# A layer of windowed and full attention beside gated experts: masks laid by ScalarE, scores in alternating banks, one store of weights, query products among the global blocks

## The chip, the cores and the metric

One NeuronCore of a Trainium2 chip runs the whole layer. The metric is the device time of one execution in microseconds; lower is better. TensorE (PE in the profile; its weight loads are PEld), VectorE (DVE), ScalarE (ACT), GpSimd (POOL) and SyncE's DMA queue (SP) each run an instruction stream of their own in order, and meet at semaphores.

## What is computed

The input x is 8 sequences of 1024 tokens with 256 features. After a layer norm, two branches are added to it:

```python
qkv = x @ w_qkv + b_qkv                      # 16 heads of 16
scores = einsum('bhqd,bhkd->bhqk', q, k) * 16 ** -0.5
scores = where(mask, -inf, scores)           # 4 global heads: j > i; 12 local heads: j > i or i - j > 64
ctx = softmax(scores) @ v;  attn = ctx @ w_out + b_out
...
xV = einsum('btd,kdr->btkr', Q_side, V)      # 8 experts of rank 64
cum_yW = cumsum(einsum('btd,kdr->btkr', K_side, W), axis=1)
weights = softmax(gelu(Q_side @ router_w1.T + b1) @ router_w2.T + b2 + expert_bias)
out = einsum('btkr,kdr->btd', xV * cum_yW * weights[..., None], U) + weights @ b
out = out / n_valid                          # once "forward", once "inverse"
...
x = x + attn(xn) + (fwd + 0.5 * inv) @ W_O.T
```

## The kernel before

**Tiling.** Work goes by 16 chunks of 512 tokens, two a sequence; `c` is a chunk's half of its sequence, so even chunks have c = 0 and odd ones c = 1. A prologue folds the weight matrices. fp32 products are made of three fp32r matmuls of high and low parts (line 676), bf16 scores of three parts stacked in 96 or 99 rows.

**The order is written out by hand.** `Plan.add` appends stages to one list, and each engine's program walks that list and issues what belongs to it. So the order of `add` is the order of every engine's queue. `weave(main, side)` spreads the groups of `side` evenly between those of `main`. `uses=[...]` claims a PSUM bank or a buffer: the user of turn n waits (`take`, or a `seed`) until turn n - 1 has been read out, which `bank_read` counts.

**A chunk** has three stages on TensorE:

1. *Peaks and experts* (line 379 on). The largest score of each query is found first: `lpeak` (12 units, line 807) and `gpeak` (10 units in an even chunk, 26 in an odd one, line 821), each a bank of scores that VectorE reduces (lines 1222 and 1229, 0.62 us a piece). They rotate through banks 4 to 7. Local ones, and global ones on the diagonal, need a mask added. TensorE adds it by a matmul with the identity (line 801), or ScalarE copies it into the bank ahead of the scores (`seed`, line 1043), which then accumulate on it. Peaks are woven in blocks of four into the expert groups. Of these each j of 8 has: `x` (query product, bank 2, line 676), which ScalarE copies to `prod` (1027) and GpSimd multiplies by gate weights broadcast in `wide` (`weigh`, 1499); `c` (product over the running sum CH, bank 3), which VectorE multiplies in (`product`, 1305) and so frees bank 3 for the next `c`; ScalarE's rounded copy PH (1037), GpSimd's rest PL (1504); and `mix` (line 787) into the output banks 0 and 1. Query products 1 and 2 of the next chunk stand at the end of the global stage.
2. *Local blocks* (`local_groups`, line 235). Three groups of four heads, each in two halves: two `lscore` pairs (line 841) in banks 5 and 6, ScalarE's exponential (1055), GpSimd's masks on the first pair (1489, 1492); the second pair has a mask laid ahead by ScalarE (1048), but for the chunk's first, where TensorE does it (835). Then `lav` (line 866) sums into a context bank, group 1 and 3 in bank 7, group 2 in bank 4, and `ctx` on VectorE transposes it out (1321). Woven in: the next chunk's transposes, its key and query parts (ScalarE 986, VectorE 1193 to 1198), then its stacks are built by DMA (1587) and its four `hidden` products follow.
3. *Global blocks* (`global_groups`, 6 in an even chunk, 14 in an odd one): `gscore` (line 880) and `gav` (line 898) in bank 4, ScalarE's exponential (1063), GpSimd's mask on the diagonal (1482). Woven in: the next chunk's gates. VectorE turns them into weights, which SP stores by four 8 KB DMAs (1630) and reads back broadcast, two DMAs a `wide` buffer (1660). Also woven in: `values` in bank 2, and `finish` (909), the attention's output product for the chunk's first half of features. Behind the last block VectorE runs `ctx` (1321 to 1325), `cturn` (1333), ScalarE `chigh` (1069), VectorE `crest` (1338), and then product 0 of the next chunk.

## Time and profile before

| | us |
|---|---|
| device time, median of 3 runs | 1487.91 (1486.12 to 1490.52) |
| the profiled execution | 1491.34 |
| its span, first to last instruction | 1489.6 |
| TensorE busy in it | 1379.5 (93%) |
| VectorE, ScalarE, GpSimd busy | 989.5, 776.1, 586.5 |
| mean granted clock of TensorE | 0.989 |

A matmul's end is modelled and overlaps the next one's start, so the cost of work on TensorE is read from start to start. A row of the timeline has start, duration, engine, line, operation, tiles, shapes and count, and in brackets the idle time of the engine before it with what ended it.

### The profile page before, as it was taken

The page shows a single profiled execution, that of the slowest core. Times are in us where ns is not written, and L with a number is a line of the kernel's source. Part 1 is how long each engine was busy: PE and PEld are TensorE (multiplying, and loading weights), DVE is VectorE, ACT ScalarE, POOL GpSimd, SP SyncE. Part 2 cuts the span into 40 slices and gives each one's busy share as a digit, 9 for nine tenths or more (in the row PEclk, how much of TensorE's full clock was granted, in tenths as well). Part 3 has the DMA queues.
Part 4 walks back from the last instruction along what each step waited for, and adds up shares of the span by engine and source line. Part 5 has one row for each costly group of instructions (what it writes and reads, how often), then busy time and mean ns, then how long its engine had stood idle before and what let it go on. Part 6 is the DMA issues. An engine that isn't in the chain of part 4 may idle for free.

```text
span 1489.6 us, 35980 instructions
## 1 busy us (share of the span) xinstructions
PE 1379.5 (93%) x14481; PEld 1035.7 (70%) x14481; DVE 989.5 (66%) x2082; ACT 776.1 (52%) x1368; POOL 586.5 (39%) x663
## 2 busy tenths in 40 slices
PE   5978999999999999999999999999999999999996
PEld 4567685777758677586856778587775868667773
DVE  6667777567756777557875677566875578656661
ACT  2434537455464735645374554646356453755544
POOL 1025343453514444253433525144452534335341
PEclk9999999999999999999999999999999999999998
DMA  8430625326062541616353171624516153431610
GB/s 189 102 94 11 168 79 127 105 65 174 25 175 70 121 126 49 166 32 151 96 123 107 40 196 30 158 87 107 141 42 163 44 146 100 118 109 42 172 40 15
DMA packets 166614, 152.88 MB, mean 103 GB/s; under 512 B 37809, under 2 KB 149808, under 8 KB 166448
## 3 DMA queue, kind: packets, MB, share of 16 engines
q1 hardware_dynamic: 166448, 150.59, 38.8%
q8 instruction: 114, 1.87, 0.5%
q14 instruction: 52, 0.43, 0.1%
HBM read 108.57 MB, written 35.65 MB: 97 GB/s over the span
## 4 chain that ended last, share of the span: by engine, by line
PE 62%; DVE 15%; ACT 8%; issue 6%; DMA 4%; POOL 2%; SPq 1%; ACTq 0%; POOLq 0%; DVEq 0%
PE PS L676 30%; PE PS L787 11%; PE PS L821 4%; DVE rest L1193 3%; PE PS L880 3%; ACT HE L1063 3%; PE PS L807 3%; PE PS L909 3%; PE PS L898 2%; PE PS L963 2%; DMA weights_d<-weights_t 2%; DVE area L1198 2%; DVE area L1196 2%; ACT HE L1055 2%; ACT PS L1048 1%
## 5 line engine op out<-in xcount | busy, mean ns | idle before, releaser
L1504 POOL TENSOR_TENSOR PL<-prod,PH 128x512 fp32r<-128x512 f32 x128 | 164.7, 1287 | 201.3 <-ACT PH L1037 201.3
L676 PE MATMUL PS<-XH,WH 128*128 128x512 f32 x512 | 218.6, 427 | 21.7 <-ACT prod L1027 10.3
L1037 ACT ACTIVATE PH<-prod 128x512 fp32r<-128x512 f32 x128 | 80.8, 632 | 268.8 <-DVE prod L1305 252.8
L1499 POOL TENSOR_TENSOR prod<-prod,rest 128x512 f32<-128x512 f32 x96 | 124.8, 1303 | 242.9 <-DMA rest<-weights_d 166.6
L1229 DVE TENSOR_REDUCE block_peak<-PS 128x4 f32<-128x512 f32 x288 | 179.8, 685 | 48.0 <-PE PS L821 47.9
L676 PE MATMUL PS<-XH,WL 128*128 128x512 f32 x512 | 204.1, 399 | 0.0
L676 PE MATMUL PS<-XL,WH 128*128 128x512 f32 x512 | 203.6, 398 | 0.0
L1482 POOL TENSOR_SCALAR_AFFINE_SELECT HE<-HE 128x256 f32<-128x256 f32 x128 | 51.2, 406 | 364.2 <-ACT HE L1063 360.6
L1063 ACT ACTIVATE HE<-PS 128x512 f32<-128x512 f32 (+1 forms) x320 | 159.9, 553 | 33.5 <-PE PS L880 30.5
L1305 DVE TENSOR_TENSOR prod<-PS,prod 128x512 f32<-128x512 f32 x128 | 87.8, 686 | 97.3 <-PE PS L676 84.5
L676 PEld LDWEIGHTS PS<-XH,WH 128*128 128x128 f32 x512 | 97.1, 190 | 63.2 <-ACT prod L1027 16.8
L787 PE MATMUL PS<-UH,PH 128*128 128x256 f32 x512 | 133.8, 294 | 2.1 <-ACT PH L1037 2.1
L1027 ACT ACTIVATE prod<-PS 128x512 f32<-128x512 f32 x128 | 75.6, 590 | 113.2 <-PE PS L676 113.2
L1222 DVE TENSOR_REDUCE peak<-PS 128x4 f32<-128x512 f32 x192 | 119.9, 682 | 13.8 <-PE PS L807 13.8
L787 PE MATMUL PS<-UL,PH 128*128 128x256 f32 x512 | 128.3, 283 | 0.0
L676 PE MATMUL PS<-CH,WH 128*128 128x512 f32 x256 | 109.3, 427 | 12.4 <-DVE prod L1305 12.4
L1321 DVE STREAM_TRANSPOSE craw<-PS 128x512 f32<-128x512 f32 x64 | 45.4, 710 | 101.7 <-PE PS L898 95.5
L676 PEld LDWEIGHTS PS<-XH,WL 128*128 128x128 f32 x512 | 96.9, 189 | 22.5
L880 PE MATMUL PS<-area 99*128 99x256 bf16 (+1 forms) x640 | 101.1, 266 | 10.4 <-ACT HE L1063 7.3
L1055 ACT ACTIVATE HE<-PS 128x512 f32<-128x512 f32 x192 | 104.9, 593 | 6.9 <-PE PS L841 6.9
L676 PEld LDWEIGHTS PS<-XL,WH 128*128 128x128 f32 x512 | 98.0, 191 | 14.8
L787 PEld LDWEIGHTS PS<-UH,PH 128*128 128x128 f32 x512 | 97.7, 191 | 7.7 <-ACT PH L1037 3.8
(186 smaller groups left out, 3064.6 us busy)
## 6 DMA issues: line engine op xcount, KB each, us to landing
parts_d<-area SPq DMA_DIRECT2D x32, 768.0 KB, 5.0
area<-parts_d SPq DMA_DIRECT2D x128, 192.0 KB, 7.9
rest<-weights_d SPq DMA_DIRECT2D x192, 128.0 KB, 3.0
area<-parts_d SPq DMA_DIRECT2D x32, 576.0 KB, 7.8
tok<-in_L_attn_x_dram SPq DMA_DIRECT2D x16, 512.0 KB, 6.2
xt<-in_L_attn_x_dram SPq DMA_DIRECT2D x16, 512.0 KB, 4.1
wide<-weights_d SPq DMA_DIRECT2D x64, 128.0 KB, 3.0
out_dram<-xt SPq DMA_DIRECT2D x16, 512.0 KB, 3.8
```

What stands on the lines that cost most here:

```text
L676: ins = e.matmul(ps, a, b, start=first and k == 0, stop=last and k == n - 1, skip_group_check=True)
L787: ins = e.matmul(out_half(t), (PH, PL)[part][:, h, t * P:(t + 1) * P], u[:, j, :], start=False, stop=False, skip_group_check=True)
L880: ins = e.matmul(psum(i, lo=HALF * a + lo, hi=HALF * (a + 1)), KG[0:KSTK, g, j * P:(j + 1) * P], QS[0:KSTK, g, half * HALF + lo:(half + 1) ...
L1027: e.activation(prod[:, j % 3, :], psum(2), ACT.Copy).then_inc(bank_read[2])
L1037: e.activation(PH[:, h, :], prod[:, j % 3, :], ACT.Copy).then_inc(phi)
L1055: e.activation(HE[:, k, :], psum(i), ACT.Exp, scale=SCALE).then_inc(bank_read[i])
L1063: e.activation(two(HE[:, k, :], lo), two(psum(i), lo), ACT.Exp, scale=SCALE).then_inc(bank_read[i])
L1222: e.tensor_reduce(peak[:, t, 4 * grp:4 * (grp + 1)], psum(i).rearrange("p (a k) -> p a k", a=4), AX_X, ALU.max).then_inc(bank_read[i])
L1229: e.tensor_reduce(block_peak[ch % NC][:, t, :, j], psum(i).rearrange("p (a k) -> p a k", a=4), AX_X, ALU.max).then_inc(bank_read[i])
L1305: e.tensor_tensor(prod[:, r, :], psum(3), prod[:, r, :], ALU.mult).then_inc(bank_read[3])
L1499: e.tensor_tensor(prod[:, j % 3, :], prod[:, j % 3, :], wide[j % WIDE], ALU.mult).then_inc(weighed)
L1504: e.tensor_tensor(PL[:, j % 2, :], prod[:, j % 3, :], PH[:, j % 2, :].bitcast(F32), ALU.subtract).then_inc(plo)
```

## The change

- Peaks start their rotation of banks anew in each chunk. In every chunk but the first, three masks of the first four local peaks are laid by ScalarE, behind the previous chunk's last global scores; the fourth stays with TensorE.
- The first local mask is laid by ScalarE ahead of the chunk's last two expert groups, and each later one a step earlier. First pairs use bank 5, second pairs 6 and 4 in turn. All three local groups sum in bank 7. Peaks are woven into all expert groups but the last two (17 instead of 19 groups behind the first, in a middle chunk).
- Query products 1 and 2 of the next chunk, and `finish` of the first half, stand among the global blocks; the first `values` stands before the last AV block in bank 7, the second behind it. The three `weigh` follow one another on GpSimd at the end.
- The gates' weights go out in one DMA of all 128 partitions (128 KB), and `wide` reads each row as two halves.
- The last global scores of a chunk, and the values, write their whole bank as TensorE sees it (scores are 256 wide instead of 128), since masks laid by ScalarE are accumulated on.
- In the first chunk, the next chunk's norm comes in one piece behind the first two peak blocks.

```diff
--- before.py
+++ after.py
@@ -112,7 +112,7 @@
     def ctx_bank(grp):
-        return 7 if grp % 2 else 4
+        return 7 if grp else 4
@@ -180,7 +180,7 @@
     def add_values(ch, u):
-        add_on("values", ch, u, uses=["bank2" if ch else f"bank{2 + u}"])
+        add_on("values", ch, u, uses=[("bank7", "bank2")[u] if ch else f"bank{2 + u}"])
         if u == T // 2 - 1:
@@ -235,15 +235,15 @@
         units = [(grp, half) for grp in range(1, 1 + NL // 4) for half in range(2)]
-        scores = [(ch, grp, half, pair, score_use()) for grp, half in units for pair in range(2)]
+        scores = [(ch, grp, half, pair, f"bank{6 - 2 * (n % 2) if pair else 5}") for n, (grp, half) in enumerate(units) for pair in range(2)]
+        masks = [[(add_seed, bank, "lscore", *key)] for *key, bank in scores[1::2]]
         order = []
         for n, (grp, half) in enumerate(units):
-            order.append([(add_lscore, *scores[2 * n]), (add_lscore, *scores[2 * n + 1])])
-            if n + 1 < len(units):
-                order[-1].append((add_seed, scores[2 * n + 3][4], "lscore", *scores[2 * n + 3][:4]))
+            order.append(masks[n + 1] if n + 1 < len(units) else [])
+            order[-1] = order[-1] + [(add_lscore, *scores[2 * n]), (add_lscore, *scores[2 * n + 1])]
             if n:
                 order[-1].append((add_lav, ch, *units[n - 1]))
-        return order
+        return order, masks[0]
@@ -258,7 +258,7 @@
         for j in range(2 * KB):
-            if j < 2 * KB - 1 and (j > 1 or not ch):
+            if 1 < j < 2 * KB - 1:
                 order.append([(add_x, ch, j + 1, part) for part in range(2)] + [(add_weigh, ch, j + 1)])
@@ -308,11 +308,12 @@
         c = ch % NC
+        turns["peak"] = 0
         order = [[(add_lpeak, ch, t, grp, peak_use())] for t in range(T) for grp in range(NL // 4)]
...
         for n, ((stage, *key),) in enumerate(order + gpeaks):
-            if stage is add_lpeak and n >= PEAKS:
+            if stage is add_lpeak and (n >= PEAKS or ch and n < PEAKS - 1):
                 masks[n].append((add_seed, key[-1], "lpeak", *key[:-1]))
@@ -320,11 +321,9 @@
         order += gpeaks
-        if ch == 0:
-            add_norm(1, order)
         blocks = range(0, len(order), PEAKS)
         joined = lambda groups, n: [stage for group in groups[n:n + PEAKS] for stage in group]
-        return [joined(order, n) + joined(masks, n + PEAKS) for n in blocks]
+        return [joined(order, n) + joined(masks, n + PEAKS) for n in blocks], joined(masks, 0)
@@ -379,17 +378,30 @@
         add_c(0, 0, part)
+    for part in range(2):
+        add_x(0, 1, part)
+    add_weigh(0, 1)
...
-        experts, peaks = expert_groups(ch), peak_groups(ch)
+        experts = expert_groups(ch)
+        peaks = next_peaks if ch else peak_groups(ch)[0]
         split = len(experts) - (0 if nxt else 4)
...
             experts[1].append((add_finish, ch - 1, 1))
-            experts[2], experts[3] = experts[3], experts[2]
-        run(experts[0] + peaks[0])
-        weave(experts[1:split], peaks[1:])
+        experts[2], experts[3] = experts[3], experts[2]
+        if ch:
+            run(experts[0] + peaks[0])
+        else:
+            run(peaks[0] + [(add_x, 0, 2, part) for part in range(2)] + [(add_weigh, 0, 2)] + peaks.pop(1))
+            for n in range(len(NORM)):
+                add("norm", 1, n)
+            run(experts[0])
+        weave(experts[1:split - 2], peaks[1:])
+        locals_, first_mask = local_groups(ch)
+        for group in [first_mask] + experts[split - 2:split]:
+            run(group)
         if ch:
@@ -402,7 +414,7 @@
             side = [[(add_rows, ch, 1)]] + experts[split:] + [last_mix]
-        weave(local_groups(ch), side)
+        weave(locals_, side)
         add_lav(ch, NL // 4, 1)
@@ -414,33 +426,36 @@
         order = global_groups(ch)
-        side = []
         if nxt:
-            first_x, first_c = ([(add, ch + 1, 0, part) for part in range(2)] for add in (add_x, add_c))
-            run(first_x + order[0] + first_c)
+            x0, x1, x2 = ([(add_x, ch + 1, j, part) for part in range(2)] for j in range(3))
+            run(x0 + order[0] + [(add_c, ch + 1, 0, part) for part in range(2)])
             add("logits", ch + 1, uses=["bank7"])
             add("chigh", ch, 0)
+            if ch + 2 < CHUNKS:
+                add_norm(ch + 2, order[1:-2])
+            steps = 2 + 3 * (ch % NC)
+            last = len(order) // 2 - 1
+            order[1] += [(add_gates, ch + 1), (add, "crest", ch, 0)]
+            for n, other in ((0, [(add_gate_parts, ch + 1)]), (steps // 2, x1), (steps, x2), (steps + steps // 2, [(add_finish, ch, 0)]),
+                             (last - 1, [(add_values, ch + 1, 0)])):
+                order[2 * n + 2] += other
+            next_peaks, first_masks = peak_groups(ch + 1)
+            order[2 * last] += first_masks
             order = order[1:]
-            if ch + 2 < CHUNKS:
-                add_norm(ch + 2, order)
-            side = [[(add_gates, ch + 1)], [(add_gate_parts, ch + 1)]] + [[]] * (2 * (ch % NC))
-            side += [[(add_values, ch + 1, 0)], [(add_values, ch + 1, 1)]]
-            side[0].append((add, "crest", ch, 0))
         else:
             add("crest", ch, 0)
-        side.append([(add_finish, ch, 0)])
-        weave(order, side)
+            order[len(order) // 2].append((add_finish, ch, 0))
+        for group in order:
+            run(group)
         if nxt:
+            add_values(ch + 1, 1)
             add("stacks", ch + 1, "global")
-        if nxt:
-            add_weigh(ch + 1, 0)
-            run([(add_x, ch + 1, 1, part) for part in range(2)])
-            add_weigh(ch + 1, 1)
         add("cturn", ch, 1)
...
         if nxt:
-            run([(add_x, ch + 1, 2, part) for part in range(2)])
-            add_weigh(ch + 1, 2)
+            for j in range(WIDE):
+                add_weigh(ch + 1, j)
         add("crest", ch, 1)
@@ -529,7 +544,7 @@
         peak_d = [nc.dram_tensor(f"peak_d_{n}", (3 * k, C), BF16, kind="Internal").ap() for n, k in (("local", NL), ("global", NG))]
-        weights_d = nc.dram_tensor("weights_d", (2 * KE, C), F32, kind="Internal").ap()
+        weights_d = nc.dram_tensor("weights_d", (P, HALF), F32, kind="Internal").ap()
         rows_d = nc.dram_tensor("rows_d", (3, 2 * KE, C), BF16, kind="Internal").ap()
@@ -717,7 +732,7 @@
                             pairs += [(xh, wh), (xh, wl), (xl, wh)]
-                        ins = mms(psum(i, lo=a * D, hi=(a + 1) * D), pairs)
+                        ins = mms(psum(i, lo=a * D, hi=(a + 1) * D), pairs, first=a == 0)
                     ins.then_inc(values_ps)
@@ -872,7 +887,7 @@
                     i, _ = where[stage]
-                    lo = max(0, (j - c * T) * P - half * HALF)
+                    lo = max(0, (j - c * T) * P - half * HALF) if (j, half) != tiles(c)[-1] else 0
                     q.wait_ge(peak_in[1], 16 * (ch + 1))
@@ -1288,7 +1303,7 @@
                     q.wait_step()
-                    q.wait_ge(weights_out, 16 * 4 * ch)
+                    q.wait_ge(weights_out, 16 * ch)
                     q.wait_ge(rows_cast, ch)
@@ -1624,10 +1639,7 @@
                         q.wait_ge(wide_in[i], 16 * 2 * (use(f"wide{i}", "wide", ch, i) - 1))
-                    for w in range(2):
-                        for h in range(2):
-                            row = 32 * (2 * w + h)
-                            e.dma_start(weights_d[KE * w:KE * (w + 1), h * HALF:(h + 1) * HALF], weights_t[row:row + KE, :]).then_inc(weights_out, 16)
+                    e.dma_start(weights_d, weights_t[:, :]).then_inc(weights_out, 16)
                     q.wait_ge(rows_cast, ch + 1)
@@ -1646,7 +1658,7 @@
                     ch, j = key
-                    q.wait_ge(weights_out, 16 * 4 * (ch + 1))
+                    q.wait_ge(weights_out, 16 * (ch + 1))
                     if j >= WIDE:
@@ -1656,8 +1668,11 @@
                             q.wait_ge(bias_in, 16 * 15)
+                    by_half = weights_d[2 * 32 * (j // KB):2 * 32 * (j // KB + 1), :].rearrange("(h e) t -> e h t", h=2)
                     for k in range(2):
-                        e.dma_start(wide[j % WIDE][R * k:R * (k + 1), :], weights_d[2 * j + k:2 * j + k + 1, :].to_broadcast([R, C])).then_inc(wide_in[j % WIDE], 16)
+                        n = 2 * (j % KB) + k
+                        e.dma_start(wide[j % WIDE][R * k:R * (k + 1), :].rearrange("p (h t) -> p h t", h=2), by_half[n:n + 1].to_broadcast([R, 2, HALF])).then_inc(wide_in[j % WIDE], 16)
```

## Rows read from the trace of the kernel before

**Rows 1.** Busy time of each engine, share of the span, instructions (the page).

```profile
PE 1379.5 (93%) x14481; PEld 1035.7 (70%) x14481; DVE 989.5 (66%) x2082; ACT 776.1 (52%) x1368; POOL 586.5 (39%) x663
```

**Rows 2.** Windows of chunks 6 and 7: stretch and length, busy us, clock, DMA.

```profile
624.01:702.35 78.34, 75.53 (x819) 59.38 (x818) 53.47 (x117) 42.66 (x74) 33.78 (x38) 1.00 0.38 96
702.35:798.21 95.86, 90.20 (x979) 65.84 (x978) 65.08 (x137) 52.09 (x92) 39.27 (x43) 1.00 0.42 114
```

**Rows 3.** TensorE's waits by releaser: us in total, times, longest.

```profile
PE PS L676 <- DVE prod L1305: 12.4, 10, 3.1
PE PS L841 <- ACT PS L1048: 11.8, 18, 0.7
...
PE PS L676 <- ACT prod L1027: 10.3, 15, 0.7
```

**Rows 4.** Timeline of TensorE, handover from chunk 7 to 8.

```profile
782.30 0.39 PE L676 MATMUL PS<-WH,XH 128*128 128x256 f32 x1
...
783.85 0.61 PE L880 MATMUL PS<-area 99*128 99x256 bf16 x4
...
790.77 0.39 PE L909 MATMUL PS<-OH,PH 128*128 128x256 f32 x1
...
792.31 0.40 PE L880 MATMUL PS<-area 99*128 99x128 bf16 x4
...
793.99 0.41 PE L898 MATMUL PS<-HE,Va 128*17 128x128 f32 x8 [0.73 <-POOL HE L1482]
...
796.69 0.50 PE L676 MATMUL PS<-XH,WH 128*128 128x512 f32 x1 [0.69 <-ACT prod L1027]
...
798.20 0.39 PE L801 MATMUL PS<-peak_mask_l,ident_b 128*128 128x512 bf16 x1
...
800.86 0.50 PE L676 MATMUL PS<-CH,WH 128*128 128x512 f32 x1
```

**Rows 5.** The same, four peak blocks without a mask of TensorE's, chunk 7.

```profile
708.78 1.08 PE L807 MATMUL PS<-area 96*64 96x128 bf16 x32
709.80 0.50 PE L676 MATMUL PS<-XH,WH 128*128 128x512 f32 x1
```

**Rows 6.** The same, the mask of the first local scores, chunk 7.

```profile
743.54 0.38 PE L835 MATMUL PS<-mask_l,ident_b 128*128 128x512 bf16 x1
743.77 0.40 PE L841 MATMUL PS<-area 99*128 99x64 bf16 x8
```

**Rows 7.** Timeline of VectorE, handover from chunk 7 to 8.

```profile
794.49 0.72 DVE L1321 STREAM_TRANSPOSE craw<-PS 128x512 f32<-128x512 f32 x1 [10.11 <-PE PS L898]
...
797.40 1.16 DVE L1338 TENSOR_TENSOR PL<-craw,PH 128x512 fp32r<-128x512 f32 x1 [0.70 <-ACT PH L1069]
798.48 0.68 DVE L1305 TENSOR_TENSOR prod<-PS,prod 128x512 f32<-128x512 f32 x1
```

**Rows 8.** Timeline of ScalarE, masks of the third block of peaks, chunk 7.

```profile
710.51 2.40 ACT L1043 ACTIVATE PS<-peak_mask_l 128x512 f32<-128x512 bf16 x4 [0.93 <-DVE peak L1222]
```

**Rows 9.** Timelines of TensorE and GpSimd, handover from chunk 6 to 7.

```profile
695.88 0.40 PE L880 MATMUL PS<-area 99*128 99x128 bf16 x4
...
705.75 0.50 PE L676 MATMUL PS<-CH,WH 128*128 128x512 f32 x1 [0.69 <-DVE prod L1305]
...
703.36 2.84 POOL L1499 TENSOR_TENSOR prod<-prod,rest 128x512 f32<-128x512 f32 x2 [5.94 <-DMA rest<-weights_d]
```

**Rows 10.** The chain that ended last, at that handover: start, us, what.

```profile
694.43 5.04 DMA weights_d<-weights_t
```

**Rows 11.** Window over the stacks' transfers: as rows 2; last are DMA share, GB/s.

```profile
684.00:697.00 13.00, 12.82 (x117) 8.63 (x116) 7.11 (x30) 10.08 (x20) 2.78 (x7) 1.00 1.10 235
```

**Rows 12.** Timelines of VectorE and TensorE, local blocks of chunk 7.

```profile
759.70 0.71 DVE L1321 STREAM_TRANSPOSE craw<-PS 128x512 f32<-128x512 f32 x1
...
758.83 0.31 PE L866 MATMUL PS<-HE,Vs 128*17 128x64 f32 x8 [0.48 <-POOL HE L1492]
...
763.86 0.50 PE L676 MATMUL PS<-XH,WH 128*128 128x512 f32 x1 [0.18 <-DVE rest L1193]
```

## The prediction, made before the changed kernel ran

> **What bounds the kernel now.** I read the page's busy times first: TensorE is busy for 93% of the span, every other engine far less [rows 1]. The windows by chunk come next: they show that an even chunk (first half of a sequence, few global blocks) takes 78.3 us and an odd one 95.9, with the granted clock at full, and that TensorE is busy for 75.5 and 90.2 of them [rows 2]. So TensorE's order of work is the time, and only three things can move it: work taken from it, waits taken from it, and waits given to it. Its waits by releaser are short and regular [rows 3]: ten for VectorE's product (12.4), fifteen, one a handover, for ScalarE's copy of a query product (10.3), eighteen for a mask laid by ScalarE (11.8). Then I read the three places that the change touches, row by row: the handover from the global blocks to the next chunk, the local blocks, and the first peaks.
>
> **Masks.** A block of four peak units with TensorE's own masks takes 800.86 - 798.20 = 2.66 us [rows 4], one without 1.02 [rows 5]: 0.41 a mask. 45 of them go (three in each chunk but the first), 18.5 us. A local mask takes the 0.23 us between its start and that of what follows [rows 6]; 16 go, 3.7 us. The last global scores grow from 0.40 to 0.61 [rows 4], 16 x 0.21 = 3.4 us more. If TensorE were never late for anything else, that alone would be 19 us. But each handover's masks lie just before the first product over CH, which waits for bank 3, and that for VectorE's product 0. So I follow who is ready when.
>
> **Handover odd to even** (7 of them). Count from the start of the last global scores. Before: 800.86 - 792.31 = 8.55 us to the first CH product [rows 4]. In it are 0.73 for GpSimd's mask, 0.69 for ScalarE's copy, two query products, the peak block with four masks. After: the wider scores and one AV block (about 1.1), the first half of the values (783.85 - 782.30 = 1.55 [rows 4]), which covers the 0.73, and the last AV block (0.35, the gap from its start to the query product's, bounded by the row's 0.41), done at about 3.1. TensorE then has the other values (1.5) and the first peak block with one mask (1.02 + 0.41): it is through at about 6.0. VectorE however still has its whole chain behind the last AV block: from the context's transpose (794.49) to the end of product 0 (798.48 + 0.68) are 4.67 us [rows 7], and the three masks (0.60 each [rows 8]) and a values copy stand before ScalarE's link of that chain, some 0.3 more. So bank 3 is free at about 8.1: **the masks, the POOL wait and the copy's wait go, and about 2 us of waiting for product 0 come.** Gain 0.45. Ahead of it two query products of 1.51 (798.20 - 796.69 [rows 4]) come in and two values go out: even. Net -0.5; bounds: -1.7 if ScalarE's queue costs nothing and the products fill waits among the global blocks, +0.4 if GpSimd's three multiplications in a row stretch VectorE's links (a subtraction beside one took 1.16, the equally wide next operation 0.68 [rows 7]). Times 7: -3.5 us.
>
> **Handover even to odd** (8). Before 705.75 - 695.88 = 9.87 us, the finish product (1.54, from 790.77 to 792.31 [rows 4]) in it [rows 9]. VectorE's chain would now end after 8.1 to 8.7 here too, but the stretch before it has finish and the two query products in and values out: +1.5. That is 0.2 or so gained or lost. The second condition is the weights: product 0 started when GpSimd's multiplication released it, and that when the broadcast rows landed [rows 9]. The last 8 KB store took 5.04 us to land [rows 10]: the DMA engines are at 1.10 of their time from 684 to 697 [rows 11], with the stacks issued before it. One store instead of four saves a microsecond of issue, into a queue that is full anyway; it carries 128 KB instead of 32, at 235 KB/us [rows 11] 0.4 us more. I take +0.15 beyond what the local stage adds, between -1.6 and +1.0; times 8: +1.2.
>
> The Trainium skill, "DMA: Bandwidth & Descriptors", section "Rules for kernel authors", says to coalesce small transfers into one, because below 64 KB mostly overhead is paid; the 5.04 us of a store of 8 KB agree that size is not what it pays for. Its section "Anatomy of one DMA" puts a DMA at about 2.0 us and its bytes at 436 GB/s: by that the single store would take an estimated 2.3 us.
>
> **Local blocks.** All three groups now gather in bank 7, where the second used bank 4. The first AV block of group 3 must wait until VectorE has transposed group 2 out of it. Before, that transpose ran from 759.70 to 760.41, behind the key parts in VectorE's queue, while that AV block started at 758.83 [rows 12]. So it starts 1.6 us later; behind it in TensorE's queue stand query parts, the last AV block and the hidden products. Those waited for VectorE themselves: the second hidden product started at 763.86 as released by VectorE [rows 12], and without that wait 0.8 us of the 1.6 remain. The alternating bank 4 takes away the 0.7 us waits for a mask (11.8 [rows 3]); but ScalarE runs the same exponentials, masks and copies there and is full, so what is late next is ScalarE itself, and AV blocks start as before. Even: +0.85. In odd chunks the last product of the experts was held up behind peaks on VectorE; with the peaks laid a group earlier about 0.5 is won: +0.3. Bounds 0 and +1.2. 8 x 0.85 + 7 x 0.3 = +8.9. In the last chunk VectorE's queue is empty there: 0.
>
> **First peaks of odd chunks.** Peaks are woven into fewer expert groups: 9 blocks into 17 where there were 19. The third block then comes right after one query product, at about 711.3 (709.80 [rows 5] + 1.51), not after the mix. Its four masks were laid from 710.51 to 712.91 [rows 8]; its fourth unit can't start before 712.9, where it would have at 712.1. 0.9 us each with its tail, 7 chunks: +6.3; bounds 0 and +1.2. The last chunk has that order already; its peaks get denser still: +1.
>
> **First chunk.** Some 6.9 of the 12.4 us of waits for products are there (the eight handovers to odd chunks have about 0.69 each [rows 9]). The new order puts chunk 1's whole norm ahead of product 0 on VectorE, and takes it out from between later products: -1.5, bounds -5 and +3.
>
> **Sum.** -3.5 + 1.2 + 8.9 + 6.3 + 1 - 1.5 = +12.4 us on the profiled execution (1491.34, span 1489.6), which is 3.4 us over the median; on the median 1487.91 that is 1500.
>
> **Rivals.** (a) **The gains land**: VectorE and ScalarE are early enough after all and TensorE's ledger is the time: masks -22.2, copy waits -10.3, POOL waits 7 x 0.73, scores +3.4, that is -34; with half of it lost to the chain, 1471. For it speaks 93% busy; against it the 4.67 us chain, which I find no way around. 0.18. (b) **The bank wait is absorbed**: the transposes come earlier in VectorE's queue, or later waits swallow it. Then the local stage is at -0.5 in odd chunks and 0 in even ones: 12.4 - 8.9 - 3.5 = 0, 1488. 0.14. (c) **One store lands early**, by the rule above, as a mechanism here: weights at hand some 2.5 us sooner, and VectorE's chain alone decides in the 8 even handovers; it is worth 0.4 each: 1497. Against it stands the full queue [rows 11]. 0.08. (d) **GpSimd's row of multiplications**: from the point where the first starts before the context's normalisation ends, that operation and the following ones take up to 0.5 to 0.7 longer at 15 handovers: 1500 + 10 = 1510, slower. The 1.16 speaks for it [rows 7], that ScalarE holds the chain meanwhile against. 0.10. The forecast itself has 0.50.
>
> The Trainium skill, "SBUF — State Buffer", section "SBUF: two separate sides", calls the port pair that VectorE and GpSimd share an exclusive lock held for a whole instruction; by that rule (d) would happen wherever a VectorE operation with two SBUF inputs meets a multiplication, and the 1.16 agrees.
>
> **How the numbers follow.** About 0.3% (4.5 us) is what a measurement of this kernel can tell from no change. Slower: forecast 0.50 less 0.04 for its lower end, (c) 0.08 less 0.02, (d) 0.10: 0.62. Same: (b) 0.14 and 0.02 from the edges: 0.16. Faster: (a) 0.18 and 0.04 of the low ends: 0.22. The terms' bounds taken half together give 1488 to 1509; the range goes to 1480, into (a), and to 1511 for (d).
>
> **What would show it.** Right: TensorE waits of about 2 us for VectorE's product 0 at every handover; AV blocks of the third local group waiting for VectorE's transpose; a wait for ScalarE's masks of 0.3 to 0.9 in the third peak block of odd chunks; the ACT copy waits gone; the store landing no sooner than the stacks. Wrong: even chunks under 78 us and odd ones under 95.5, which would mean that VectorE's chain starts or runs earlier than its row says.

## The result, and the profile after

The changed kernel takes 1539.12 us (median of 4 runs, 1537.46 to 1542.07) against 1487.01 of the kernel before beside it: ratio 1.0352, 95% interval 1.0322 to 1.0381. It is slower, as forecast, but by 52 us and not by 12, and outside the range. The profiled execution took 1540.33, span 1538.6. Lines of the code after are 15 higher than before from the matrix helper on (L676 is now L691).

Busy times and TensorE's waits (releaser, us in total, times, longest), where [rows 1] and [rows 3] stood:

```profile
PE 1385.8 (90%) x14420; PEld 1054.1 (69%) x14420; DVE 980.0 (64%) x2082; ACT 797.6 (52%) x1429; POOL 580.4 (38%) x663
```

```profile
PE PS L691 <- DVE prod L1320: 47.3, 23, 9.3
PE PS L881 <- DVE craw L1336: 44.7, 30, 2.3
...
PE PS L856 <- ACT HE L1070: 8.7, 16, 1.1
...
PE PS L822 <- ACT PS L1058: 1.8, 10, 0.2
```

The fifteen waits for ScalarE's product copy and the eighteen for its masks at the local scores are gone, but for one of 0.3 us, as the change meant. In their place stand 47.3 us for VectorE's products and 44.7 for its context transposes. But TensorE also has 61 instructions fewer and is busy for 6 us longer. The windows by chunk (columns as in [rows 2]) show why: the granted clock, 1.00 in both before, is 0.98 and 0.97.

```profile
638.61:721.23 82.62, 75.98 (x816) 60.45 (x815) 55.50 (x118) 44.47 (x80) 33.52 (x38) 0.98 0.41 103
721.23:819.32 98.09, 91.38 (x976) 67.81 (x975) 63.95 (x136) 53.12 (x96) 38.49 (x44) 0.97 0.40 103
```

TensorE at the handover from chunk 7 to 8, as in [rows 4], the same product behind chunk 8, and the window just behind the first of them:

```profile
814.70 0.61 PE L895 MATMUL PS<-area 99*128 99x256 bf16 x4
...
818.00 0.38 PE L691 MATMUL PS<-WH,XH 128*128 128x256 f32 x1
...
820.74 0.41 PE L822 MATMUL PS<-area 96*64 96x128 bf16 x8
823.38 0.50 PE L691 MATMUL PS<-CH,WH 128*128 128x512 f32 x1 [2.23 <-DVE prod L1320]
...
824.23 0.63 PE L691 MATMUL PS<-CH,WH 128*128 128x512 f32 x1
...
906.38 0.80 PE L691 MATMUL PS<-CH,WH 128*128 128x512 f32 x1 [2.51 <-DVE prod L1320]
```

```profile
824.11:827.52 3.41, 3.41 (x15) 3.02 (x14) 2.72 (x5) 2.24 (x4) 1.24 (x1) 0.50 0.50 154
```

From the last scores to the first product over CH (tokens) are 8.68 us (8.55 before), 2.23 of them a wait. Then the same matmul takes 0.63 us instead of 0.40: the granted clock has dropped to its lower level, 1.2 GHz, and stays there for 3.41 us. The trace has 7 such stretches before, one of them between chunk 0 and the last chunk, and 26 after. In the middle chunks each stands in or just behind a wait: the one above, at 12 of the 15 handovers, or one of those in the local blocks, where TensorE waits for VectorE to transpose contexts out of their bank (`craw`):

```profile
953.86 0.42 PE L881 MATMUL PS<-HE,Vs 128*17 128x64 f32 x8 [1.13 <-DVE craw L1336]
...
963.55 0.31 PE L881 MATMUL PS<-HE,Vs 128*17 128x64 f32 x8 [1.42 <-DVE craw L1336]
```

The wait alone does not settle it. At the handover to chunk 14 it is 2.23 us too, and the clock behind it stays at 1.00:

```profile
1367.70 0.50 PE L691 MATMUL PS<-CH,WH 128*128 128x512 f32 x1 [2.23 <-DVE prod L1320]
```

```profile
1367.70:1371.11 3.41, 3.41 (x32) 3.01 (x34) 3.41 (x6) 3.20 (x6) 1.30 (x1) 1.00 0.69 180
```

By phases of the trace, as a mean of a chunk (seven even, seven odd; "head" is from the first peak scores, without a mask ahead of them, to the first local scores or their mask, and has the end of the handover in it):

| us | head even, odd | local even, odd | global even, odd | chunk 0 | last chunk |
|---|---|---|---|---|---|
| before | 36.01, 41.07 | 25.33, 26.28 | 17.00, 28.94 | 89.89 | 86.00 |
| after | 39.30, 43.37 | 26.78, 27.55 | 16.51, 27.27 | 92.67 | 89.45 |

### The profile page after: what moved, and what is told of

Its sections match the earlier page's. It is cut to its first block, busy times and chain, and to the rows that moved or that the text cites. A ratio compares the mean times of both kernels' runs of the same rounds, so it can differ in the third digit from the quotient of the medians.

```text
span 1538.6 us, 35861 instructions
## 1 busy us (share of the span) xinstructions
PE 1385.8 (90%) x14420; PEld 1054.1 (69%) x14420; DVE 980.0 (64%) x2082; ACT 797.6 (52%) x1429; POOL 580.4 (38%) x663
## 4 chain that ended last, share of the span: by engine, by line
PE 66%; DVE 17%; ACT 6%; issue 5%; DMA 4%; POOL 2%; SPq 0%; ACTq 0%; DVEq 0%; POOLq 0%
PE PS L691 32%; PE PS L802 11%; PE PS L836 4%; PE PS L881 3%; PE PS L895 3%; PE PS L913 3%; PE PS L924 3%; DMA weights_d<-weights_t 2%; ACT HE L1078 2%; PE PS L978 2%; DVE area L1211 2%; DVE craw L1336 2%; DVE rest L1208 2%; DMA rest<-weights_d 1%; PE PS L822 1%
## 5 line engine op out<-in xcount | busy, mean ns | idle before, releaser
L691 PE MATMUL PS<-XH,WH 128*128 128x512 f32 x512 | 222.5, 435 | 4.4 <-DVE XL L1184 1.9
L691 PE MATMUL PS<-XL,WH 128*128 128x512 f32 x512 | 207.1, 404 | 0.0
L691 PE MATMUL PS<-XH,WL 128*128 128x512 f32 x512 | 206.5, 403 | 0.0
L691 PE MATMUL PS<-CH,WH 128*128 128x512 f32 x256 | 112.3, 439 | 47.3 <-DVE prod L1320 47.3
L691 PEld LDWEIGHTS PS<-XH,WH 128*128 128x128 f32 x512 | 99.5, 194 | 41.8 <-issue 13.0
L691 PEld LDWEIGHTS PS<-XH,WL 128*128 128x128 f32 x512 | 99.2, 194 | 23.9
L691 PEld LDWEIGHTS PS<-XL,WH 128*128 128x128 f32 x512 | 100.2, 196 | 16.1
L691 PE MATMUL PS<-CH,WL 128*128 128x512 f32 x256 | 107.6, 420 | 0.0
L1058 ACT ACTIVATE PS<-peak_mask_l 128x512 f32<-128x512 bf16 x173 | 101.1, 600 | 11.8 <-DVE peak L1237 11.6
```

The lines of the kernel that those rows point to most:

```text
L691: ins = e.matmul(ps, a, b, start=first and k == 0, stop=last and k == n - 1, skip_group_check=True)
L1058: e.activation(psum(i).rearrange("p (a k) -> p a k", a=4), local_peak_mask(*of[1:3]), ACT.Copy).then_inc(seeded)
```

## The experiments

Theory C: the new waits cost twice, themselves and a stretch at half clock. Theory D: they cost themselves, and the clock falls for other reasons. The kernel before ran beside all of them; ratios are against it.

**Work put into the handover's wait** (from the changed kernel).

```diff
+            add("fill", ch, uses=["bank2"])
...
+                elif kind == "fill":
+                    take(2, *stage)
+                    for n in range(8):
+                        ins = e.matmul(psum(2), WH[:, 0, COL_X:COL_X + P], XH[:, 0, :], start=True, stop=True, skip_group_check=True)
+                    ins.then_inc(bank_read[2])
```

> The changed kernel with eight 128x512 matmuls more, at 0.21 us each, in the gap before each chunk's first product of tokens (15 gaps of 2.2 to 2.5 us behind the last peak block, while the first product of weights is not ready). Their results are used by nothing. Theory C (the clock): a wait of TensorE here costs itself and then a stretch of 3.41 us at half clock that begins within a microsecond of its end, some 1.7 us of work lost each time. With work in the gap the wait's end stays where it was, the stretch goes, and the time falls though work is added: 1539 less 15 x 1.7, about 1514, with some 15 half-clock stretches fewer than the 26 of the changed kernel. Theory D (the dependencies alone; the clock falls whatever TensorE does just then): 1539, or up to 1545 where the eight matmuls end after the product is ready.

Measured: 1518.15 us, ratio 1.0228 (1.0194 to 1.0263). The same handover, and the window behind it:

```profile
809.88 0.41 PE L829 MATMUL PS<-area 96*64 96x128 bf16 x8
810.22 2.14 PE L784 MATMUL PS<-XH,WH 128*128 128x512 f32 x8
812.52 0.50 PE L692 MATMUL PS<-CH,WH 128*128 128x512 f32 x1 [0.16 <-DVE prod L1327]
```

```profile
812.52:815.93 3.41, 3.41 (x32) 3.01 (x34) 3.41 (x6) 3.19 (x6) 1.29 (x1) 1.00 0.65 189
```

The first product over CH comes 8.67 us after the last scores (803.85), as late as without the eight matmuls. The clock behind it is at 1.00, and the kernel is 21 us faster for 120 matmuls more. Only C gives that. The handovers held 13 lengths of 3.41 us (one stretch is twice as long), so each cost 1.6 us. The changed kernel shows the same by itself: the head of chunk 14, without a stretch, takes 38.02 us, those of the other even chunks 39.50 to 39.53. But only 8 of the 26 stretches are gone in all, where 15 were expected: 18 are left, the middle ones now in the local blocks.

The Trainium skill, "TensorE: Matmul & The Clock Gate", section "HAM oscillation — how this bites in real kernels", puts the penalty of a throttled time at half of it, which would be 1.7 us of 3.41. The 1.5 to 1.6 us measured here nearly agree.

**Local stage as before** (from the changed kernel).

```diff
-        return 7 if grp else 4
+        return 7 if grp % 2 else 4
...
-        scores = [(ch, grp, half, pair, f"bank{6 - 2 * (n % 2) if pair else 5}") for n, (grp, half) in enumerate(units) for pair in range(2)]
+        scores = [(ch, grp, half, pair, f"bank{6 if pair else 5}") for n, (grp, half) in enumerate(units) for pair in range(2)]
...
-            order.append(masks[n + 1] if n + 1 < len(units) else [])
-            order[-1] = order[-1] + [(add_lscore, *scores[2 * n]), (add_lscore, *scores[2 * n + 1])]
+            order.append([(add_lscore, *scores[2 * n]), (add_lscore, *scores[2 * n + 1])])
+            if n + 1 < len(units):
+                order[-1] += masks[n + 1]
```

> The changed kernel with the local stage as it was before: context banks 7 and 4 in turn, one bank for the second pair of local scores, each mask laid behind the scores of the block ahead of it. The first mask of a chunk stays where the change put it. Theory C (waits and the clock behind them): the 30 waits for craw at line 881, 44.7 us in all, go; the waits for ScalarE's reading of the score banks come back (11.8 us before), with some 6 us of waits for GpSimd that were hidden behind the craw waits; and the eight half-clock stretches inside the odd chunks' local stages go, 8 x 1.7 us. About 1498. Theory D (waits alone): the stretches stay or cost nothing, about 1512. Theory E (the waits only stand in for others of the same length, those for gathered inputs): 1530 or more.

Measured: 1507.65 us, ratio 1.0145 (1.0115 to 1.0175): 31 us less, between C and D. The waits for craw are gone, 12.1 us for ScalarE's masks are back. A local stage takes 25.08 us (even) and 25.29 (odd), which is 1.7 and 2.3 less, 28 us in 14 chunks. It is also 0.25 and 1.0 less than in the kernel before (25.33 and 26.28), 9 us in 14 chunks. I put that down to what this kernel keeps of the change there, the first mask laid by ScalarE and the last two expert groups free of peaks; neither was tried alone. 14 of the 15 handovers have a half-clock stretch.

**Queries' products back behind the global stage** (from the changed kernel).

```diff
-            for n, other in ((0, [(add_gate_parts, ch + 1)]), (steps // 2, x1), (steps, x2), (steps + steps // 2, [(add_finish, ch, 0)]),
+            for n, other in ((0, [(add_gate_parts, ch + 1)]), (steps + steps // 2, [(add_finish, ch, 0)]),
...
+            add_weigh(ch + 1, 0)
+            run(x1)
+            add_weigh(ch + 1, 1)
...
-            for j in range(WIDE):
-                add_weigh(ch + 1, j)
+            run(x2)
+            add_weigh(ch + 1, 2)
```

> The changed kernel with the queries' products 1 and 2 of the next chunk back behind the global stage, beside their weighings, as before. Theory C: their 12 matmuls of 128x512, some 2.6 us for each product, fill the gap of 2.2 to 2.5 us ahead of the first product of tokens, and leave the global stage, which gets shorter by what they took there: 15 x 2.4 us less, and 15 stretches at half clock less, 15 x 1.7. About 1478. Theory D (waits alone): 1503. Theory F (the first product of weights is late because of the order in which the weighings reach GpSimd and VectorE, so that it moves later by what is put ahead of it): 1530 to 1545.

Measured: 1515.36 us, ratio 1.0194 (1.017 to 1.0217). The handover's waits for product 0 are gone outside the first chunk (11.8 us where 47.3 were), but two others stand there, 12.3 us for ScalarE's copy of the values (0.82 each) and 10.3 for its copy of a query product, which C had left out: hence 24 us won and not 61. And the stretches that had been behind these waits now stand in the local blocks, one in each chunk.

**Both at once.**

> Both edits at once, the local stage as before and the queries' products at the end of the global stage; what is left of the change are the masks of first maxima laid by ScalarE, the values' bank, the weights stored at once, and the order of the first chunk. Theory C: the two gains add, and the granted clock is back near 0.99: 1440 to 1460. Theory D (waits alone): about 1476. If the two edits take away the same loss (a wait removed at one place shows up at the next), less than their sum: 1475 to 1490.

Measured: 1483.29 us (10 runs), ratio 0.9969 (0.995 to 0.9987). The two edits give 31 and 24 us apart and 56 together: they add. No half-clock stretch is left between chunk 0 and the last chunk. The 1440 to 1460 counted gains whose place other waits take.

**Parts of the change alone, on the kernel before.** First the queries' products among the global blocks, their weighings behind them:

```diff
+            steps = 2 + 3 * (ch % NC)
+            for n, j in ((steps // 2, 1), (steps, 2)):
+                order[2 * n + 1] += [(add_x, ch + 1, j, part) for part in range(2)]
...
-            add_weigh(ch + 1, 0)
-            run([(add_x, ch + 1, 1, part) for part in range(2)])
-            add_weigh(ch + 1, 1)
...
-            run([(add_x, ch + 1, 2, part) for part in range(2)])
-            add_weigh(ch + 1, 2)
+            for j in range(WIDE):
+                add_weigh(ch + 1, j)
```

> The kernel before with one part of the change: products 1 and 2 of the next chunk's queries among the global blocks, the three weighings in a row behind. Theory C: the first product of weights is ready some 8.7 us after the last scores whatever stands there; TensorE has about 4.5 us of other work, so it waits some 3.5 us and loses 1.7 more at half clock, while the global stage grows by the 3.0 us of the two products: 15 x 4.7 less 15 x 0.7 (the wait between the two products, gone) = 60 us, about 1545. Theory D: the product of weights moves forward as far as its queue gets shorter; only the difference seen between the changed kernel and the one with the queries moved back comes, 24 us: 1512.

Measured: 1560.41 us, ratio 1.048 (1.045 to 1.051), the slowest of all. Its waits for the product, and a window around the end of such a wait (735.50):

```profile
PE PS L675 <- DVE prod L1304: 59.4, 18, 5.2
```

```profile
733.06:739.89 6.83, 4.39 (x14) 3.81 (x15) 4.84 (x9) 3.62 (x6) 1.28 (x1) 0.52 0.59 175
```

The 3 us of products leave the handover. Behind an odd chunk TensorE's first product over CH comes 1.5 us sooner (7.07 us behind the last scores, 8.55 before), after a wait of 2.30. Behind an even one it mostly comes later (10.0 to 10.8 us but in the last chunk, mostly 9.3 to 10.1 before), and the longer wait there, 4.4 to 5.2 us but in the last chunk, now brings twice the stretch at half clock. In the full change the values moved behind the last scores fill part of that hole.

Then the changed local stage, in which the first mask is laid only behind the last expert group; and then its one bank, of which this is the whole edit:

```diff
-        return 7 if grp % 2 else 4
+        return 7 if grp else 4
```

> The kernel before with the changed local stage alone: context bank 7 for three of the four groups, the second pair's banks 6 and 4 in turn, each mask laid a block ahead, the first by ScalarE's side of the plan. Theory C (waits and the clock behind them): two waits for craw in each chunk, about 1.2 us each, in place of the short waits for ScalarE and GpSimd, net some 18 us, and a stretch at half clock in each chunk that the kernel before doesn't have, about 14 more, 14 x 1.7 us less what they overlap: 1515 to 1530. Theory D (waits alone): 1506. Theory A (as I predicted, one wait in each chunk): 1488 + 9 = 1497 or less.

Measured: 1528.65 us, ratio 1.0284 (1.0266 to 1.0303). Its waits, and one for ScalarE's first mask in chunk 7:

```profile
PE PS L868 <- DVE craw L1323: 48.2, 30, 2.3
PE PS L843 <- ACT PS L1050: 18.0, 16, 1.7
```

```profile
760.73 0.41 PE L843 MATMUL PS<-area 99*128 99x64 bf16 x8 [1.71 <-ACT PS L1050]
```

> The kernel before with one line of the change: bank 7 for the local contexts of all three groups, where bank 4 served the second. Masks and score banks stay as they were. Theory K (the one bank is what the changed local stage costs): about 30 waits for craw, two in each chunk, 1.0 to 2.3 us each, and the whole of the 40 us that the changed local stage alone costs: 1520 to 1530. Theory M (the order of masks and score banks is what puts the contexts behind VectorE): one wait a chunk as I predicted, 1488 to 1500.

Measured: 1514.11 us, ratio 1.0184 (1.0164 to 1.0205).

```profile
PE PS L866 <- DVE craw L1321: 23.5, 21, 2.0
```

The shared context bank costs 27 of the 41 us, its waits and the half-clock stretches at them together. The other 14 come with the masks and score banks as they are laid here: the waits for craw double, and those for ScalarE's masks, 11.8 before, grow to 18.0 rather than go. This loss is in the odd chunks, whose local stage takes 30.80 us (28.17 with the one bank alone); the even ones take 27.27 (27.57). The change lays the first mask two groups earlier, has a single wait for a mask in the local blocks, of 0.3 us, and takes 27.55 in odd chunks, so these 14 us can't be carried over to it. There the 28 us that came back with the old local stage are about what the bank costs alone in the same 14 stages, 29 us. The Trainium skill, "Perfetto Trace Analysis", section "Matmuls", wants independent groups rotated through PSUM banks so that the reading of one overlaps the next; the 27 us for one bank fewer agree.

Two masks of the first peaks laid by ScalarE:

> The kernel before with one part of the change: the masks of two of a chunk's first peak blocks laid by ScalarE in the global stage ahead, with the peak banks starting over at each chunk and the last scores of a chunk at full width. Theory A (the ledger holds): two masks less on TensorE, 15 x 2 x 0.23 us, so 1481. Theory B (they stand in the handover, and the first product of weights is what ends it): the time given back is waited for again ahead of the first product of tokens, 1488 or up to 3 us more. Theory C (that new wait pulls the clock down): 15 stretches of 3.41 us at half clock more, 1510.

Measured: 1483.61 us, ratio 0.9975 (0.9961 to 0.9989): 4 us won, between A and B. An even chunk takes 77.83 us (78.34 before), an odd one 96.30 (96.29): where VectorE's product 0 is waited for already, fewer masks buy nothing.

One store of the weights:

> The kernel before with one part of the change: the weights stored by one transfer of 128 rows in place of four. As predicted, the store ends with the transfers of the stacks around it and lands no sooner, and its readers' many short pieces cost the handover from odd to even chunks 0.15 us each: 1488 to 1490. If four stores were the limit: 7 handovers x 0.5 to 1 us less, 1481 to 1484.

Measured: 1492.12 us (11 runs), ratio 1.0035 (1.0021 to 1.0049). Median time from issue to landing of the wide reads, before and in this kernel, and of the one store:

```profile
rest<-weights_d SPq DMA_DIRECT2D x192, 128.0 KB, 3.0
```

```profile
rest<-weights_d SPq DMA_DIRECT2D x192, 128.0 KB, 3.4
...
weights_d<-weights_t SPq DMA_DIRECT2D x16, 128.0 KB, 6.0
```

The one store lands no sooner than the 5.04 us of an 8 KB one [rows 10], and its readers are 0.4 us slower in half rows. It is no gain, but a loss, by the interval of 3 to 7 us. By chunks the middle ones account for 3 us of it, all in the odd ones: 96.70 us (96.29 before); an even chunk takes 78.34 as before.

**What ends the handover's wait** (from the changed kernel).

```diff
-            run(experts[0] + peaks[0])
+            run(experts[0])
+            add("crest", ch - 1, 1)
+            run(peaks[0])
...
-        add("crest", ch, 1)
+        else:
+            add("crest", ch, 1)
```

> The changed kernel with VectorE's product of weights 0 ahead of the previous chunk's last rest of the contexts (two instructions of 0.69 us that stand in the other order in the change, of which the first waits for ScalarE). Theory H (behind an even chunk VectorE's own order ends the wait, behind an odd one the weights' way through memory and GpSimd does): the first product of tokens comes 1.3 us earlier in 8 handovers and not at all in 7: 10 us less, and more if the shorter waits no longer pull the clock down there (up to 8 x 1.7): 1515 to 1529. Theory F (GpSimd's multiplication sets both, or the finish of the chunk before waits for the rest instead): 1536 to 1542.

Measured: 1527.61 us, ratio 1.0258 (1.0219 to 1.0297), 11.5 us less than the change. My text had the two kinds of handover the wrong way round. In the changed kernel VectorE goes from the rest straight into the product behind odd chunk 7, and waits for GpSimd's multiplication behind even chunk 8:

```profile
822.03 0.69 DVE L1353 TENSOR_TENSOR PL<-craw,PH 128x512 fp32r<-128x512 f32 x1 [0.70 <-ACT PH L1084]
822.64 0.69 DVE L1320 TENSOR_TENSOR prod<-PS,prod 128x512 f32<-128x512 f32 x1
...
905.63 0.69 DVE L1320 TENSOR_TENSOR prod<-PS,prod 128x512 f32<-128x512 f32 x1 [1.15 <-POOL prod L1514]
```

With the order turned, the wait behind chunk 7 is 0.80 instead of 2.23:

```profile
816.55 0.50 PE L694 MATMUL PS<-CH,WH 128*128 128x512 f32 x1 [0.80 <-DVE prod L1323]
```

The head of an even chunk gets 2.6 us shorter, 1.4 of waiting and the rest clock; that of an odd one doesn't. Part is given back in the even chunks' local blocks (27.64 for 26.78), where the stretch at half clock then comes.

**Work put into the local wait** (from the kernel with the queries' products moved back): the same fill, nine matmuls into bank 3, ahead of the third group's contexts. The lines of the fill itself are as above, but for the bank and the count.

```diff
+            if n == 5:
+                order[-1].append((add_fill, ch, n))
```

> The kernel with the queries' products moved back (1515; its half-clock stretches, one in each chunk, begin in the wait of 2.3 us for craw at the third group of local contexts), with nine 128x512 matmuls of 0.21 us more in that wait, their results used by nothing. Theory C (the clock falls because TensorE waits): 14 of its 20 half-clock stretches go, 14 x 1.7 us, about 1491, though 16 x 1.9 us of work are added. Theory D (the waits cost their own length and no more): 1515, or up to 8 more where the nine matmuls end late.

Measured: 1514.53 us, ratio 1.0164 (1.0131 to 1.0197): no gain. Waits for craw, with and without the fill (first without):

```profile
PE PS L884 <- DVE craw L1339: 37.3, 30, 2.3
```

```profile
PE PS L895 <- DVE craw L1350: 15.6, 15, 1.1
```

Ten of 20 half-clock stretches went, so the fill does keep the clock up; but the time is D's. Chunk by chunk the reason shows. The local stages that have no stretch any more got shorter: even ones take 26.60 us, where they took 26.63 to 28.15 with a stretch in each, and odd ones 27.02, where most took 27.7. But six middle ones still have a stretch, now always at the second group's wait, which is not filled, and these take 27.9 (even) and 28.4 (odd): 1.3 to 1.4 us more than their like without one in the same kernel. The two effects cancel.

So a stretch in the local blocks costs from nothing to 1.5 us. What it delays shortens the next wait, if there is one: in the kernel with the handover's wait filled, an even local stage takes 26.51 us with a stretch at the second group's wait and 26.59 without any, as the third group's wait shrinks from 2.28 to 0.66 us. With the fill there is no third wait left to take it up. Nor did the stretches without the fill all begin where the text above has them: in only three of the middle chunks they stand at the third group's wait, in the others at the second group's. In even chunks the former take 28.0 and 28.2 us, the latter 26.6 to 27.2.

**First chunk: the norm behind product 0** (from the kernel with both edits).

```diff
-            for n in range(len(NORM)):
-                add("norm", 1, n)
             run(experts[0])
+            add_norm(1, peaks)
```

> As the kernel with local stage and queries back, and in chunk 0 the first product of weights ahead of the norm of chunk 1, whose steps are spread among the peak blocks as before. Theory C: VectorE's norm, 7 us from its statistics to its last scaling, stood ahead of product 0 and held TensorE for 9.7 us; the wait falls to about 2, as before, and the 10.24 us at half clock that begin there shrink too: 1483 less 8 to 12, about 1473. Theory G (the norm is late for chunk 1 instead, or the peaks' reading is delayed by it): 1481 to 1485.

Measured: 1477.6 us (8 runs), ratio 0.9944 (0.9926 to 0.9962). (This kernel is the "e10" of the next expectation.) The wait of 9.7 us went, and the product waits are 7.1 us in all where they were 13.2. The 10.24 us at half clock in chunk 0 stayed, against what was expected.

**One query product on each side** (from that kernel): x1 among the global blocks, x2 behind.

> As e10, with product 1 of the next chunk's queries among the global blocks and product 2 behind them. Theory C: the handover from the last scores to the first product of tokens takes 11.2 us with both queries' products behind the scores, and the first product of weights can be ready 8.7 us after the last scores; one of the two moved away brings it to about 9, for 1.5 us more in the global stage: 15 x (2.2 less 1.5) = 10 us less than e10, no wait of over a microsecond, no more stretches at half clock, about 1463. Theory F: product 0 comes later with it, the wait is back and the clock falls behind it: 1490 or more.

Measured: 1470.96 us, ratio 0.9889 (0.9867 to 0.9911), faster than the kernel before and the changed one, by 6.6 us on the last step where C had 10 or more. The first product over CH comes 8.87 us behind the last scores, without a wait at that row:

```profile
779.90 0.61 PE L897 MATMUL PS<-area 99*128 99x256 bf16 x4
...
785.71 0.50 PE L693 MATMUL PS<-XH,WH 128*128 128x512 f32 x1 [0.82 <-ACT Va L1015]
...
788.77 0.50 PE L693 MATMUL PS<-CH,WH 128*128 128x512 f32 x1
```

Two attempts at the waits that are left, product 0 ahead of the rest of the contexts, and with it x2 moved between the last scores and the last contexts:

> The same edit on the fastest kernel so far (local stage as before, one queries' product on each side, norm later: 1471). There TensorE finds work up to 8.9 us behind the last scores and waits 0.3 us for product 0, 15 times. Every theory: 1466 to 1471, no half-clock stretch more; it tells whether that wait is worth anything at all.

Measured: 1478.49 us, ratio 0.993 (0.9906 to 0.9954): 7.5 us lost, which no theory had. By chunks the loss is in the heads of the odd ones (41.98 us, 40.66 without the edit); even chunks take the same. Waits for ScalarE's masks at the peaks rise from 2.8 to 8.3 us and make up most of it. What holds the masks back was not tested.

> The kernel with one query product on each side of the last scores and product 0 ahead of the rest of the contexts, and with the second query product moved between the last scores and the last contexts. The wait of 0.82 us for ScalarE's reading of the values (15 times) and the short one for the last scores' exponentials are then covered by it: 15 x 0.8 = 12 us less, about 1463. If the chain from the last contexts through VectorE comes late instead and TensorE waits for it behind the first product of tokens, a new wait of about 1.5 us: 1475 or more, with half-clock stretches.

Measured: 1481.99 us (12 runs), ratio 0.9966 (0.9952 to 0.9981): no gain over that either, by chunks within 0.1 us of it (79.05 and 95.34 us; 79.01 and 95.28). The wait for the values became one for the copy of x2, which frees the same bank:

```profile
783.43 0.39 PE L698 MATMUL PS<-WH,XH 128*128 128x256 f32 x1 [1.06 <-ACT prod L1049]
```

And the store, on the fastest kernel, on one chip with and without:

> The kernel with one query product ahead (1471), with the weights stored by four transfers and the wide reads in whole rows, as before the change. If the 4.6 us that the single store alone cost the kernel before are its own price (wide reads in half rows land 0.4 us later, 3.4 against 3.0), it is 3 to 5 us faster than the same kernel with one store, run beside it: 1466 to 1468. If that difference was in the runs and not in the store, the two are within 1.5 us of each other.

> The kernel with one query product ahead once more, unchanged, beside the one above: 1468 to 1474, or up to 1478 if the 1471 owed something to its chip.

Measured: 1467.03 us with four stores, ratio 0.9856 (0.9842 to 0.9869), and 1468.49 with one, ratio 0.9879 (0.9859 to 0.9899). The two times can't be told from each other by their intervals. The traces tell more, since much of the variation from run to run lies in the start and in the first and last chunk. The kernel with one store has an even middle chunk at 79.00 us in both of its traces and an odd one at 93.98 and 93.97 in the mean; with four stores they are 79.02 and 93.45. Single odd chunks spread by up to 0.8 us, but the head takes at most 40.12 us in six of the seven with four stores, and at least 40.32 in all fourteen with one. So the single store costs 0.5 us at a handover to an odd chunk in this kernel, and 0.4 in the kernel before: 3 to 4 us at eight of them. The version with four stores, 1.4% faster than the kernel before, is the best of the case.

## Why the prediction was wrong in size

The step that failed is at the start: "only three things can move it: work taken from it, waits taken from it, and waits given to it". The speed at which TensorE works was a fourth. I read 1.00 in [rows 2] as a constant, and it was a result of an order without long waits. The trace of the kernel before already had the sign. I took the handovers to odd chunks for waits of 0.69 us each; they range from none to 1.94, and the one of 1.94, in chunk 5, just outside the two chunks of [rows 2], has a stretch at half clock behind it:

```profile
530.01 0.50 PE L676 MATMUL PS<-CH,WH 128*128 128x512 f32 x1 [1.94 <-DVE prod L1305]
```

```profile
530.91:534.32 3.41, 3.41 (x15) 3.13 (x14) 2.80 (x5) 2.08 (x4) 3.02 (x3) 0.50 0.65 168
```

That chunk takes 98.66 us, the other odd ones 95.5 to 96.3. Of the 2.8 us more, 1.2 are the longer wait; the other 1.5 or so fit the clock. Term by term, on the two spans (together +49.0 where I had +12.4):

| term | predicted | measured | why |
|---|---|---|---|
| handover odd to even, 7 | -3.5 | +11.3 (head +3.29, global -1.67) | wait right, clock missed |
| handover even to odd and third peak block | +7.5 | +12.7 (head +2.30, global -0.49) | clock missed, block over-sized |
| local blocks, 14 | +8.9 | +19.0 | a second wait, and clock; the rest of the stage gained |
| last chunk | +1 | +3.5 | its own handover |
| first chunk | -1.5 | +2.5 (with the start of the span) | norm ahead of product 0 |

- **Handovers.** The wait was foreseen at its place and nearly at its size: "about 2 us of waiting for product 0" were 2.23 and 2.51, the first CH product at 8.1 was at 8.68. The 0.6 has the shape of rival (d): the normalisation beside GpSimd's multiplication took 1.38 us behind chunk 7 and 0.42 behind chunk 8, where none ran. Not foreseen was what follows the wait at 12 of the 15 handovers: 1.5 to 1.6 us of lost clock for each 3.41 us, 21 us in all by the filled wait, more than half of the miss of 37.
- **Local blocks.** "So it starts 1.6 us later" named one wait a chunk, at group 3. There are two (30 waits, 44.7 us), at groups 2 and 3: group 2 waits for group 1 in bank 7 as well, which the code before would have shown, since group 1 sat there already. And "the alternating bank 4 takes away the 0.7 us waits for a mask" came true. The 19 us are a sum of two: the shared bank at +28, of which the sum had one wait at 0.85 us or less, and what else changed there at -9 (25.08 and 25.29 us with the old banks in the changed kernel, 25.33 and 26.28 before), of which it had 0.5 in odd chunks. The trace of the change also parts waits from clock. Its even local stages without a stretch take 26.6 us and its one odd stage without a stretch 27.00, which is 14 us over the kernel before in 14 chunks; the seven stages with one take 0.6 to 1.3 more, some 5 us. The odd share rests on that one stage, and on one more without a stretch, of 27.02, in the kernel with the handover's wait filled.
- **Third peak block**: 0.18 us where I had 0.9. Its fourth unit did find its mask late (the 0.18 us waits for ScalarE above), but the block came 7.0 us behind the first product over CH (chunk 9) where I had 5.6, so that hardly anything was left of the wait; of the 6.3 us for seven chunks about 1 came.
- **First chunk.** The norm was taken for a gain from its later places; ahead of product 0 it holds TensorE for 9.26 us. Put behind, with both other edits in, it gave 6.
- **Store, masks.** The store landed no sooner, as said, and cost 0.4 to 0.5 us a handover to an odd chunk where the sum had 0.15 beside the rest. Of the masks of the first peaks two of three were tried alone: about 7 us of TensorE's work bought 4 in time, none of it where the handover ends with VectorE. The third, and what all three are worth in the change, was not tested.
- Rivals (a) and (b) fell with the waits. (c) fell with the store's 6.4 us to landing in the changed kernel (6.0 alone), where the estimate was 2.3. (d) came true in part: the normalisation took 1.36 to 1.39 us at all seven handovers from odd to even chunks (0.42 before), and not at seven of the other eight.

What stays open: why the same wait of 2.2 us is followed by a half-clock stretch at most handovers and not at all of them.

## What to carry to other kernels

Work next to a dependency is cover. Before moving it away, count what then stands between the last producer and the wait, and price the wait with what the granted clock does behind it, not by its length alone; windows at clock 1.00 say only that their own order has no such waits, so look for the window that reads less. If a wait can't be removed, even useless matmuls in it can pay (21 us here), unless a later wait would have taken up the delay anyway.

To price a small edit, compare the middle chunks of two traces beside the two medians: here even chunks repeat to some hundredths of a microsecond and the mean of the odd ones to some tenths, where the whole time varies by several.

A PSUM bank shared by groups that follow each other makes each group wait for the reader of the last one, behind whatever that reader has queued.

## What the runs showed that I had not expected

- At 12 of 15 handovers a wait of TensorE of 2.05 to 3.54 us between dense matmuls came with 3.41 us at 1.2 GHz or twice that (granted clock 0.50 in that window, 128x512 matmuls at 0.63 us for 0.40), which cost 21 us. At the other three, with waits of 2.23, 2.51 and 2.65 us, the clock stayed up. Waits of 0.69 and 0.82 us in the middle chunks of the kernels without the long ones had no such stretch behind them.
- Such a stretch moves: where the handover's wait was removed, the stretch came at the next wait in the local blocks, one in each chunk, and only with both gone it was gone.
- What a stretch costs depends on what comes behind it: 1.3 to 1.6 us ahead of dense work, next to nothing where the next wait of TensorE takes up the delay.
